# Attention scores of two heads in one fp32 matmul instead of two

## The reference, cut to what matters

```python
# x: 32 batches x 64 rows x 512; 32 query heads, 8 key/value heads, head size 128
q = (layernorm(x) @ Wq.T)      # 32 heads
k = (ctx @ Wk.T)               # 8 heads, each shared by 4 query heads
q = rmsnorm(q) * q_norm_w;  k = rmsnorm(k) * k_norm_w
scores = einsum("bhqd,bhkd->bhqk", q, k) / sqrt(128) + mask
out = softmax(scores) @ v      # then @ Wo.T, a gated residual, and the expert layer
```

## Time and profile before

| | |
|---|---|
| time, median of 3 runs | 1530.38 us (1528.94 to 1534.23) |
| span of the profiled execution | 1529.2 us (the profile gives no other time of its own) |
| TensorE busy in the span | 1447.3 us (95%) |
| weight loads busy | 1245.8 us (81%) |
| VectorE, ScalarE, GpSimd busy | 60%, 40%, 36% |
| attention steps | about 14.59 us each, from 222 to 1155 us |

### The profile page before, as it was taken

One profiled execution on the slowest core, in us unless ns is written; L12 is line 12 of the kernel. 1 busy time (PEld: TensorE's weight loads), 2 busy tenths in 40 slices (PEclk: granted clock), 3 DMA queues, 4 the chain that ended last, 5 costly groups with the idle time before them and its releaser, 6 DMA issues.

```text
span 1529.2 us, 34430 instructions
## 1 busy us (share of the span) xinstructions
PE 1447.3 (95%) x11630; PEld 1245.8 (81%) x11631; DVE 912.5 (60%) x1903; ACT 611.0 (40%) x1322; POOL 546.1 (36%) x599
## 2 busy tenths in 40 slices
PE   6999989999999999999999999999996999999980
PEld 5888878889898898898988989889885888777750
DVE  5444446667666676666666766667889532244435
ACT  4333344444454444544444445444454411222210
POOL 1222234333433433334333343343442061233335
PEclk9999999999999999999999999999998999999995
DMA  6534431111111111101111111111123183355547
GB/s 214 159 117 131 127 104 39 34 38 36 35 40 33 38 38 36 38 31 40 38 34 39 31 38 39 34 38 53 59 78 133 42 171 105 118 170 165 165 157 255
DMA packets 92758, 125.71 MB, mean 82 GB/s; under 512 B 9010, under 2 KB 58209, under 8 KB 92193
## 3 DMA queue, kind: packets, MB, share of 16 engines
q1 hardware_dynamic: 85360, 104.21, 22.4%
q0 software_dynamic: 7344, 20.73, 4.8%
HBM read 87.39 MB, written 37.53 MB: 82 GB/s over the span
## 4 chain that ended last, share of the span: by engine, by line
PE 89%; DVE 3%; POOL 3%; DMA 2%; issue 2%; ACT 0%; SPq 0%; POOLq 0%; DVEq 0%
PE ps L515 23%; PE ps L517 21%; PE ps L516 21%; PE ps L796 5%; PE ps L582 4%; PE ps L627 4%; PE ps L812 3%; PE ps L594 2%; POOL y L495 2%; PE ps L613 2%; PE ps L791 1%; PE ps L563 1%; DMA acc<-in_wv 1%; DMA wgu<-in_w_gu 1%; DVE h L1275 0%
## 5 line engine op out<-in xcount | busy, mean ns | idle before, releaser
L515 PE MATMUL ps<-hT,w0h 128*128 (+2 forms) x640 | 198.5, 310 | 2.3 <-issue 1.5
L516 PE MATMUL ps<-hT,w0l 128*128 (+2 forms) x640 | 195.1, 305 | 0.0
L517 PE MATMUL ps<-hT,w0h 128*128 (+2 forms) x640 | 195.1, 305 | 0.0
L427 POOL TENSOR_TENSOR sq<-sq,sqb 128x512 f32<-128x512 f32 x64 | 75.3, 1176 | 317.7 <-ACT sqb L930 317.7
L436 POOL TENSOR_TENSOR qr<-qv,mhalf 128x8 f32<-128x8 f32 x64 | 105.2, 1643 | 224.3 <-DVE qv L1163 224.3
L961 ACT CAST ah<-ps 128x256 fp32r<-128x256 f32 x256 | 84.3, 390 | 180.3 <-PE ps L517 177.6
L515 PE MATMUL ps<-hT,w1h 128*128 (+1 forms) x512 | 147.3, 288 | 0.0
L516 PE MATMUL ps<-hT,w1l 128*128 (+1 forms) x512 | 144.8, 283 | 0.0
L517 PE MATMUL ps<-hT,w1h 128*128 (+1 forms) x512 | 144.7, 283 | 0.0
L515 PEld LDWEIGHTS ps<-hT,w0h 128*128 128x128 f32 x640 | 122.7, 192 | 9.4 <-issue 2.3
L516 PEld LDWEIGHTS ps<-hT,w0l 128*128 128x128 f32 x640 | 122.8, 192 | 6.0
(11 more groups left out here) (217 smaller groups left out, 3668.0 us busy)
## 6 DMA issues: line engine op xcount, KB each, us to landing
wraw<-in_w_att SPq DMA_DIRECT2D x64, 256.0 KB, 2.6
ybuf<-ye SPq DMA_DIRECT2D x47, 256.0 KB, 2.0
vbuf<-vo SPq DMA_DIRECT2D x16, 512.0 KB, 3.3
kbuf<-ko SPq DMA_DIRECT2D x16, 512.0 KB, 4.0
kt<-kbuf SPq DMA_DIRECT2D x64, 128.0 KB, 2.0
vt<-vbuf SPq DMA_DIRECT2D x64, 128.0 KB, 2.0
wgu<-in_w_gu SPq DMA_DIRECT2D x4, 2048.0 KB, 12.8
craw<-in_ctxT SPq DMA_DIRECT2D x9, 512.0 KB, 4.9
```

The costliest lines, as they stand in the source:

```text
L427: pool.tensor_tensor(flat(sq[:, 0]), flat(sq[:, 0]), part[0], ALU.subtract).then_inc(sq_pool, 1)
L515: pe.matmul(dst, l_hi, r_lo, start=first, stop=False)
L516: pe.matmul(dst, l_lo, r_hi, start=False, stop=False)
L517: return pe.matmul(dst, l_hi, r_hi, start=False, stop=last)
```

## The change

The two matmuls of a pair become one: stationary are the 2 x 64 query rows of both heads (`qs[:, hp, b]`, which lie next to each other), 128 columns; moving are the same 64 keys; the output covers all 128 partitions. The values land where they did. 8 matmuls in a step instead of 16.

```diff
@@ def scores(j):
                 for hp in range(2):
                     for b in range(CB):
-                        for h in range(2):
-                            mm = pe.matmul(PS[3][h * S:(h + 1) * S, (CB * hp + b) * S:(CB * hp + b + 1) * S],
-                                           qs[:, hp, b, h], kt[:, b, :], start=True, stop=True)
+                        mm = pe.matmul(PS[3][:, (CB * hp + b) * S:(CB * hp + b + 1) * S],
+                                       qs[:, hp, b].rearrange("p h s -> p (h s)"), kt[:, b, :],
+                                       start=True, stop=True)
                 mm.then_inc(s_done, 1)
```

## The result

The changed kernel takes 1572.72 us, the median of 4 runs (1572.12 to 1575.22), against 1531.49 us before (4 runs, 1528.94 to 1534.23). The ratio is 1.0269, 95% interval 1.025 to 1.0288: slower by 41 us. 1572.4 was predicted.

What follows compares the result with a forecast made beforehand. TensorE was taken to bound the attention; 63 steps of +0.68 us less 0.8 us absorbed gave +42.0 us, a span of 1571.2 us and, with 1.2 us from span to median, 1572.4 us; range 1560 to 1590 us.

Steps and rivals of the forecast that it cites:

- What bounds the kernel: In the attention TensorE is busy 910.8 of 916 us, so what the change adds to its step lengthens the span.
- the busy time of TensorE's matmul rows: Sign in the profile after: this busy time falls or stays while the span grows.
- The slot: In the scores, each load of 128 stationary columns takes 0.11 us, with the 64 moving columns (0.058 us) hidden under the next.
- The two slots that would have carried rivals, 0.06 and 0.17 us: Scores' load spacing: 0.06 if loads are fast (chance 0.09), 0.17 if load and pass run one after the other (0.07).
- The entry: From `probs_v` to the scores, 0.32 us between loads, costed as staying the same.
- the way out: From the scores' last load to the projection's first: the 0.15 us change from half arrays to whole counted as gained.
- The sum: Scores grow from 1.08 to 1.76 us, +0.68 a step; 63 steps give 42.8 us, less 0.8 absorbed: +42.0 us.
- The steps at the end: In the last 4 steps TensorE waits about 0.19 us for the squares, so 0.8 us of the added time is absorbed.
- Fast loads: Rival: 128-column score loads at 0.06 us a slot, -0.12 us a step, -7.6 us, 1523 us; chance 0.09.
- The transposes' price: Lower bound for a 128-column load in the scores: the small transposes' loads start 0.06 us apart.
- The halves at the same time: In the scores before, the two heads' passes run together in array halves, a pair in 0.058 us; the change gives this up.

Runs made afterwards that it cites:

- The two longer moving sizes: Changed kernel with 6 of 8 score matmuls a step moving 128 key columns: 1.0272 of before; with every one moving 256: 1.0972.
- the 96 columns: Changed kernel with 96 instead of 128 stationary columns in the score matmuls: 1.0104 of before.
- The run with one pair: Kernel before with the change for the first pair of heads alone, 4 matmuls of 128 stationary columns, then 8 of 64: 1.0191 of before.
- the run with quarters: Kernel before with each score matmul cut into two of 32 stationary columns, neighbours in the four quarters of the array: 0.9986 of before.
- the heads apart: Kernel before with, for each pair, all four batches of the first head's scores ahead of the second's: 1.014 of before.
- one change of half: Kernel before with all 8 score matmuls of the first heads first, then all 8 of the second: 1.0279 of before.
- quarters for the first pair: Kernel before with only the first pair of score matmuls of a step cut into four of 32 stationary columns: 1.0038 of before.

## Why the prediction was right

**What bounds the kernel.** Right. The attention grew by 41.9 us, the median by 41, and TensorE's waits did not grow. One of the signs that were to show it was wrong: the busy time of TensorE's matmul rows was to fall or stay, and it rose by 46 us (1447.3 to 1493.5). The new rows are 0.275 us long and start 0.111 apart, so they overlap and cover the whole longer stretch. A busy share of TensorE made of such rows does not tell a load that limits from a pass that limits; the distances of the starts do.

**The slot.** 0.11 us was taken, 0.111 measured. The two longer moving sizes showed that it is the load and not the pass, and the 96 columns that it goes by the column. The Trainium skill's P / 1.2 ns ("TensorE: Matmul & The Clock Gate", "LDWEIGHTS (loading the stationary operand)") gives 80 and 107 ns for 96 and 128 columns; the distances measured are 84 and 111, so it holds with 4 to 5 ns added. The two slots that would have carried rivals, 0.06 and 0.17 us, did not occur: the length of a row of loads, 141 against 190 ns, was the right sign that a transpose's load is another thing than a plain one.

**The ways in and out.** The entry was costed as unchanged, 0.32 us, and is. On the way out 0.15 us were counted as gained, and the projection's load now follows after 0.11 us. The run with one pair put the 0.15 us back.

**The sum.** 0.68 us a step was forecast, 0.70 is found between the loads and 0.71 between the steps (15.30 - 14.59). 63 times that is 45 us, 2 more than the forecast's 42.8. That the sum still hit to within a microsecond is luck: a term of nearly the same size was missing. TensorE's steps stand in an outer loop of 16, and at its two turns (within the 17th and the 33rd step) the kernel before waits for nothing that the profile shows, as here, in the timeline of its matmuls:

```profile
463.02 0.39 PE L517 MATMUL ps<-w1h,ah 128*128 128x512 f32 x1
464.27 0.38 PE L515 MATMUL ps<-hT,w0h 128*128 128x256 f32 x1 [0.86 <-issue]
```

These two steps were 15.70 and 15.46 us long, 2.0 us over the others, and in the changed kernel both are 15.30 like the rest. So 44.7 - 2.0 - 0.8 = 41.9 us. Without that luck the forecast would have been some 2 us off, still well within its range; I had seen the row in the list of waits and put no change on it. The instruction queue's line on the page (packets, MB, share), first before, then after:

```profile
q8 instruction: 40, 0.66, 0.2%
```

```profile
q8 instruction: 21, 0.34, 0.1%
```

All five kernels with 21 packets (the changed one, both with more moving columns, 96 columns, one pair) have no such wait, and all five with 40 or more have it, so it goes with the longer instruction stream. How long it is does not follow from the number of instructions: 2.1 us together in the run with quarters (46 packets), 1.5 in the kernel before, but 0.8 and 0.5 with the heads apart and with one change of half, which have the same 40 packets and as many instructions as before, and 0.4 with quarters for the first pair (41 packets). That TensorE waits there for its instructions is likely and not shown. The steps at the end, 14.80 us before, are 15.30 after, so they took up 0.2 us each, as forecast.

**The rivals.** Fast loads would have needed 0.0675 us a slot or less; by 0.8 to 0.9 ns a column that would be reached at about 75 stationary columns (an estimate), not at 128. The transposes' price does not carry over.

**The halves at the same time.** Right, and it is the reason for the loss. But I described it as pairs of neighbours meeting in a slot. The two runs with other orders show more: TensorE goes three passes ahead across halves.

## What to carry to other kernels

Before merging small matmuls, compare what sets their slot: the load by stationary columns (0.11 us for 128 in plain fp32) against the pass by moving columns (0.84 ns each in plain fp32). Here, with 64 moving columns, two matmuls of 64 stationary columns in different halves of the array load and multiply at the same time and cost 0.058 us a pass together; one of 128 costs 0.111, so half as many instructions took 1.78 us instead of 1.08. At 128 moving columns the wide form still takes 0.111 us a slot and at 256 columns 0.215, the pass's own time. So from about 128 on it should cost no more than the halves; no run here had halves with so many moving columns, so this is an estimate. Where the arrangement changes between halves, quarters and the whole array, it cost about 0.15 us each time.

## What was not expected of the hardware

Matmuls in different halves of the array overtake: with all passes of one head ahead of the other's, 23 slots sufficed for 32 passes and three changes of half, and 29 for one change, where strict order needs 29 and 31. The number of slots shows it, and so does the place of the rows of 270 ns, three passes early at each change. The Trainium skill ("TensorE: Matmul & The Clock Gate", Part 3, "The mechanism") calls matmuls strictly in order at start and end; the two runs here don't agree with that for starts in different halves of the columns. Four quarters run at once as well as two halves, with a pass started every 0.015 us on average, less than the 0.025 us between the sums of squares.
